# The end of a graph attention kernel: range check moved into the last row group, last accumulators' large halves added from PSUM, last row group stored in four

## The chip, the cores and the metric

One core of a Trainium2 chip. The metric is the device time of one execution in microseconds, the median of several runs. Profile times are microseconds from the start of the span; an engine's idle time stands in square brackets behind an instruction, with what ended it.

## The reference

The input is x, 8192 rows of 128, an adjacency matrix adj of 8192 x 8192 integers 0 or 1 with about 0.2% ones, a 128 x 128 matrix W and a vector a of 256.

```python
h = relu(layernorm(x))
Wh = h @ W
f1, f2 = Wh @ a[:128], Wh @ a[128:]
e = leaky_relu(f1[:, None] + f2[None, :], 0.2)
e = where(adj == 0, -inf, e)
out = x + softmax(e, axis=1) @ Wh
```

## The kernel before

The 8192 rows are 64 tiles of 128 (NB), in 16 row groups of four (NQ = 16, PACK = 4). The columns are walked in 16 units of 512 (UN = 16). The exponentials of the attention are written as a maximum of two products, so that the weight of an edge is the larger of a row factor and a column factor, times the edge's mark; `weights` (line 784) forms them on VectorE, four operations of 128x512 for each unit, reading the row factors from a bank of the PSUM tensor `stage` and writing to `wt_ring`, which holds two units (NW = 8).

TensorE's `unit` waits for a unit's weights and runs `products`: for each of the four row tiles r, eight matmuls (lines 376 and 380) add to `acc[:, r]`, one PSUM bank for each row tile. The factors are kept as a large and a small half in 16 bits: columns 0 to 128 of a bank (E1 = 129: 128 features and the sum of weights) collect the large part, columns 129 to 257 the small one, scaled by LOW = 2048. Ahead of most units stand two transposes of adjacency words (line 365), which ScalarE turns into marks (line 541). VectorE may write the weights of unit u once TensorE has finished unit u - 2 (semaphore `used`).

At the end of a row group ScalarE copies the four accumulators to `fin` (`evacuate`, line 576). For groups 0 to 14 the sum of the two halves, the division and the addition of x run on GpSimd, VectorE and ScalarE beside the next group, and SP stores the group's 256 KB (line 176).

For the last group it is done at once, on VectorE: for each row tile r it waits for ScalarE's copy (`acc_free`), adds the halves (line 880), takes the reciprocal of the sum of weights (line 882) and forms the output in `xm` (line 884). Then SP stores the whole group with one transfer.

The factors of the fast way are only valid for inputs in a certain range. `lim` holds, for each partition, the largest f2, the largest -f2 and a sum of squares. After the last unit TensorE turns it into one partition with three matmuls against the identity (line 457; each runs as two passes); VectorE then reduces these and compares them in four small operations (lines 870 to 874), before it takes up the last group's sums, and writes `flag`. Each engine loads the flag into a register; with these inputs it is 1, and the exact but slow way behind `Else` isn't run. The helper `then` makes VectorE wait until the operation just issued has completed.

The order on each engine is written out by hand, and the engines meet at semaphores. Engine queues: SP stores, GpSimd loads adjacency.

Of the kernel before, what the change touches and what calls it, by code (L numbers as in the profile page):

```python
# [28 lines left out]
ALU = mybir.AluOpType  # L29
ACT = mybir.ActivationFunctionType  # L30
# [8 lines left out]
P = 128  # L39
PACK = 4  # L40
# [19 lines left out]
def gat_kernel(nc, x, adj, W, a, out):  # L60
# [20 lines left out]
    with ExitStack() as ctx:  # L81
# [83 lines left out]
        @block.sync  # L165
        def _(sp):
            def load_x(k):
                lo, hi = BATCHES[k]
                sp.dma_start(xm[:, lo:hi, :], x_dram[:, lo:hi, :]).then_inc(x_loaded[k], 16)

            for k in range(len(BATCHES)):
                load_x(k)

            with sp.Fori(0, NQ) as q:
                sp.wait_ge(s["rows_done"], (q + 1) * PACK)
                sp.dma_start(out_dram[:, q, :], xm[:, q, :]).then_inc(s["out_stored"], 16)
            sp.wait_ge(s["flag_ready"], 1)
            fast = sp.value_load(flag[0:1, 0:1], min_val=0, max_val=1)
            sp.wait_ge(s["out_stored"], 16 * NQ)
            with sp.If(fast):  # L180
                pass
            with sp.Else():
                sp.dma_start(xm[:], x_dram).then_inc(s["x_again"], 16)
                with sp.Fori(0, NQ) as q:
                    sp.wait_ge(s["rows_done"], NB + (q + 1) * PACK)
                    sp.dma_start(out_dram[:, q, :], xm[:, q, :]).then_inc(s["out_stored"], 16)
                sp.wait_ge(s["out_stored"], 16 * 2 * NQ)


        @block.gpsimd  # L190
# [132 lines left out]
        def _(pe):  # L323
# [125 lines left out]
            for b in range(UN):  # L449
# [1 line left out]
                    pe.wait_ge(s["marked"], (NQ - 1) * UN + b + 2)  # L451
                    transposes(b + 2, (NQ - 1) * UN + b + 2)
                unit((NQ - 1) * UN + b, b, NQ - 1)
            pe.wait_ge(s["limits_ready"], 1)
            pe.wait_ge(s["weighted"], NQ * UN * PACK)
            for k in range(3):
                mm = nc.tensor.matmul(stage[0:1, 0, k * P:(k + 1) * P], lim[:, k:k + 1], ident[:],
                                      start=(k == 0), stop=(k == 2), skip_group_check=True)
            mm.then_inc(s["limits_turned"], 1)
            pe.wait_ge(s["flag_ready"], 1)  # L460
            fast = pe.value_load(flag[0:1, 0:1], min_val=0, max_val=1)
            with pe.If(fast):
                pass
            with pe.Else():
                pe.wait_ge(s["acc_free"], NB)
                pe.wait_ge(s["weighted"], NQ * UN * PACK)
                for q in range(NQ):
                    if q >= 4:
                        pe.wait_ge(s["row_ready"], q - 3)
                    for r in range(PACK):  # L470
                        t = q * PACK + r
                        mm = nc.tensor.transpose(acc[:, q % 4, r * P:(r + 1) * P],
                                                 wh[:, t, E1:WC].to_broadcast([P, P]), ident[:])
                    mm.then_inc(s["rowp_ready"], 1)
                pe.wait_ge(s["row_ready"], NQ)
                with pe.Fori(0, NQ) as q:
                    for n in range(GC):
                        c, at = n // PACK, q * GC + n
                        pe.wait_ge(s["g_probs"], at + 1)
                        for k in range(KC):  # L480
                            for r in range(PACK):
                                mm = nc.tensor.transpose(stage[:, k, r * P:(r + 1) * P], scoreq[:, k, r, :], ident[:])
                            mm.then_inc(s["g_tp"], 1)
                        for k in range(KC):
                            pe.wait_ge(s["g_t"], at * KC + k + 1)
                            for r in range(PACK):
                                mm = nc.tensor.matmul(acc[:, 0, 0:Fo], probt[:, k, r * P:(r + 1) * P],
                                                      wh[:, (c * KC + k) * PACK + r, 0:Fo],
                                                      start=(k == 0 and r == 0),
                                                      stop=(k == KC - 1 and r == PACK - 1))  # L490
                        mm.then_inc(s["g_sums"], 1)
# [3 lines left out]
        def _(act):  # L495
# [182 lines left out]
            for b in range(2, UN):  # L678
                steady(NQ - 1, b, more=b + AHEAD < UN)
                if b == 8:  # L680
                    divided(NQ - 2)
            evacuate(NQ - 1)
            act.wait_ge(s["flag_ready"], 1)
            fast = act.value_load(flag[0:1, 0:1], min_val=0, max_val=1)
            with act.If(fast):
# [19 lines left out]
        def _(dve):  # L705
            steps = [0]

            def then(ins):

                steps[0] += 1  # L710
                ins.then_inc(s["dve_step"], 1)
                dve.wait_ge(s["dve_step"], steps[0])
# [117 lines left out]
            for b in range(UN):  # L830
# [12 lines left out]
                if b == 3 or b == 7:  # L843
                    inverses(3 + b // 7)

            def rows(q, bank, more=True):

                dve.wait_ge(s["e_kept"], q)
                if more:
                    next_group(q + 1)  # L850
                for b in range(UN):
                    u = q * UN + b
                    dve.wait_ge(s["marked"], u + 1)
                    dve.wait_ge(s["used"], u - 1)
                    weights(bank, b)
                    if b == 6:
                        dve.wait_ge(s["sums_ready"], q)
                        nc.vector.reciprocal(inv[:], fin[:, :, Fo]).then_inc(s["inv_ready"], 1)

            f2 = wh[:, :, E1]  # L860
            nc.vector.reduce_max(lim[:, 0:1], f2, AX_X)
# [2 lines left out]
            with dve.Fori(0, (NQ - 2) // 2) as p:  # L864
                rows(p * 2 + 1, 2)
                rows(p * 2 + 2, 1)
            rows(NQ - 1, 2, more=False)
            dve.wait_ge(s["limits_turned"], 1)
            square_limits = [v * v / (NORM * D) for v in WH_LIMITS]
            then(nc.vector.reduce_max(glim[0:1, :], stage[0:1, 0, 0:3 * P].rearrange("p (k i) -> p k i", k=3), AX_X))  # L870
            then(nc.vector.tensor_scalar(gs[0:1, 0:1], glim[0:1, 0:1], glim[0:1, 1:2], F2_LIMIT, ALU.max, ALU.is_le))
            then(nc.vector.tensor_scalar(gs[0:1, 1:2], glim[0:1, 2:3], square_limits[1], gs[0:1, 0:1],
                                         ALU.is_le, ALU.mult))
            nc.vector.tensor_scalar(flag[0:1, :], glim[0:1, 2:3], square_limits[0], gs[0:1, 1:2],
                                    ALU.is_ge, ALU.mult).then_inc(s["flag_ready"], 1)

            q = NQ - 1
            for r in range(PACK):
                dve.wait_ge(s["acc_free"], q * PACK + r + 1)
                then(nc.vector.scalar_tensor_tensor(out=fin[:, r, 0:E1], in0=fin[:, r, E1:2 * E1], scalar=1.0 / LOW,  # L880
                                                    in1=fin[:, r, 0:E1], op0=ALU.mult, op1=ALU.add))
                then(nc.vector.reciprocal(inv[:, r:r + 1], fin[:, r, Fo:E1]))
                o = xm[:, q, r * P:(r + 1) * P]
                nc.vector.scalar_tensor_tensor(out=o, in0=fin[:, r, 0:Fo], scalar=inv[:, r:r + 1], in1=o,
                                               op0=ALU.mult, op1=ALU.add).then_inc(s["rows_done"], 1)
# [82 lines left out]
```

## Time and profile before

| | |
|---|---|
| median of 3 runs | 836.5 us (836.43 to 836.5) |
| the profiled execution's own time | 836.72 us |
| its span | 835.1 us |
| TensorE busy (matmul) | 790.1 us, 95% |
| VectorE busy | 758.2 us, 91% |
| ScalarE busy | 487.9 us, 58% |
| GpSimd busy | 411.2 us, 49% |
| granted TensorE clock, mean | 0.991 of full speed |

PE is TensorE's matmuls, PEld its weight loads, DVE is VectorE, ACT ScalarE, POOL GpSimd, SPq SP's queue. The ends of matmuls are modelled: they overlap, so the distance between two starts, not the duration, is the price of one in a stream.

### The profile page before, as it was taken

What the parts mean: (1) busy time and instruction counts of PE and PEld (TensorE: products, weight loads), DVE (VectorE), ACT (ScalarE), POOL (GpSimd) and SP (SyncE); (2) the same over time, 40 slices, a digit from 0 to 9 for tenths busy, and PEclk for the clock granted to TensorE, in tenths of its full rate; (3) what the DMA queues carried; (4) which work ended last, traced back from release to release, by engine and by line L of the source; (5) the groups of instructions that cost most, each with busy time, mean ns of one, the idle gap of its engine ahead of it and who ended that gap; (6) DMA issues with size and microseconds to landing.
All of it is one profiled execution on the core that took longest, in us unless ns stands there. A gap on an engine that the chain in (4) does not pass through costs nothing.

```text
span 835.1 us, 22635 instructions
## 1 busy us (share of the span) xinstructions
PE 790.1 (95%) x8969; PEld 722.9 (87%) x8969; DVE 758.2 (91%) x1243; ACT 487.9 (58%) x793; POOL 411.2 (49%) x606
## 2 busy tenths in 40 slices
PE   3578989999999999999999999999999999999995
PEld 2467879999999999999999999999999999999995
DVE  4699999999999999999999999999999999999995
ACT  4477975555565555555565555555565556555541
POOL 4655656554554446554554446554554446553410
PEclk9899999999999999999999999999999999999998
DMA  9997579999999999999999999999999999997200
GB/s 222 116 108 69 51 73 105 105 87 98 98 90 101 88 107 87 101 87 98 96 90 101 87 106 89 101 87 102 95 88 101 87 109 84 103 86 80 27 15 16
DMA packets 43281, 75.99 MB, mean 91 GB/s; under 512 B 4720, under 2 KB 6896, under 8 KB 43248
## 3 DMA queue, kind: packets, MB, share of 16 engines
q0 software_dynamic: 38400, 67.13, 87.2%
q1 hardware_dynamic: 4432, 8.39, 2.9%
q8 instruction: 17, 0.28, 0.1%
q10 hardware_dynamic: 416, 0.07, 0.0%
q14 instruction: 16, 0.13, 0.0%
HBM read 272.70 MB, written 4.19 MB: 332 GB/s over the span
## 4 chain that ended last, share of the span: by engine, by line
PE 85%; DVE 7%; DMA 4%; ACT 2%; issue 1%; POOL 1%; ACTq 0%; DVEq 0%; POOLq 0%
PE acc L376 51%; PE acc L380 26%; PE stage L365 6%; DMA masks<-in_adj_dram 4%; DVE wt_ring L784 4%; DVE pairs L774 1%; DVE packed L766 1%; PE stage L356 1%; DVE stats L719 1%; ACT masks L559 0%; DVE packed L765 0%; PE stage L348 0%; ACT marks L541 0%; ACT wh L519 0%; ACT pairs L596 0%
## 5 line engine op out<-in xcount | busy, mean ns | idle before, releaser
L784 DVE SCALAR_TENSOR_TENSOR wt_ring<-stage,packed,marks 128x512 f32<-128x512 f32 x1024 | 697.7, 744 | 47.9 <-PE acc L380 41.9
L376 PE MATMUL acc<-pairs,wt_ring 128*128 128x258 f16 x4096 | 721.2, 274 | 9.1 <-DVE pairs L774 8.7
L380 PE MATMUL acc<-pairs,wt_ring 128*128 128x129 f16 x4096 | 699.6, 219 | 0.0
L376 PEld LDWEIGHTS acc<-pairs,wt_ring 128*128 128x128 f16 x4096 | 396.9, 97 | 65.1 <-issue 8.6
L541 ACT ACTIVATE marks<-stage 128x1024 uint16<-128x1024 uint8 x256 | 261.9, 1023 | 292.5 <-PE stage L365 291.5
L380 PEld LDWEIGHTS acc<-pairs,wt_ring 128*128 128x128 f16 x4096 | 400.4, 98 | 2.5
L193 POOL DMA_DIRECT2D masks<-in_adj_dram x252 | 137.7, 549 | 329.7 <-PE stage L365 306.7
L215 POOL TENSOR_TENSOR masks<-masks 128x256 int32<-128x256 int32 x256 | 179.5, 738 | 14.5 <-ACT masks L559 13.6
L559 ACT ACTIVATE masks<-masks 128x512 uint16<-128x512 uint16 x252 | 156.4, 622 | 8.3 <-DMA masks<-in_adj_dram 8.3
L365 PE MATMUL stage<-ident,masks 128*128 128x128 f32 x512 | 99.5, 276 | 2.6 <-ACT fin L632 2.0
L365 PEld LDWEIGHTS stage<-ident,masks 128*128 128x128 f32 x512 | 54.2, 142 | 6.3 <-ACT fin L632 2.3
L348 PE MATMUL stage<-wx,ht 128*128 128x130 f32 x128 | 24.9, 325 | 11.1 <-ACT wh L519 10.4
L348 PEld LDWEIGHTS stage<-wx,ht 128*128 128x128 f32 x128 | 19.8, 220 | 13.7 <-ACT wh L519 12.0
L576 ACT ACTIVATE fin<-acc 128x258 f32<-128x258 f32 x64 | 21.2, 388 | 9.5 <-PE acc L376 9.5
L251 POOL TENSOR_TENSOR tmp<-wh,tmp 128x512 f32<-128x512 f32 x15 | 16.3, 1085 | 19.0 <-ACT tmp L532 18.9
L258 POOL TENSOR_SCALAR fin<-fin 128x516 f32<-128x516 f32 x15 | 22.9, 1524 | 0.3
L268 POOL TENSOR_TENSOR xm<-fin,xm 128x512 f32<-128x512 f32 x15 | 18.0, 1203 | 3.0 <-ACT fin L582 2.9
L582 ACT ACTIVATE fin<-fin,inv 128x128 f32<-128x128 f32 x60 | 19.0, 390 | 0.0
L774 DVE SCALAR_TENSOR_TENSOR pairs<-pairs,tmp 128x516 f16<-128x516 f16 x16 | 13.7, 857 | 5.5 <-ACT pairs L596 5.5
L519 ACT ACTIVATE wh<-stage 128x260 f32<-128x260 f32 x32 | 12.2, 381 | 9.9 <-PE stage L348 9.6
L261 POOL TENSOR_TENSOR fin<-fin 128x516 f32<-128x516 f32 x15 | 16.6, 1104 | 1.3
L335 PE MATMUL stage<-ident,xn 128*128 128x128 f32 x64 | 12.0, 321 | 5.3 <-ACT xn L504 5.3
(62 smaller groups left out, 161.1 us busy)
## 6 DMA issues: line engine op xcount, KB each, us to landing
masks<-in_adj_dram POOLq DMA_DIRECT2D x256, 256.0 KB, 7.1
out_dram<-xm SPq DMA_DIRECT2D x16, 256.0 KB, 7.5
xm<-in_x_dram SPq DMA_DIRECT2D x3, 1024.0 KB, 15.5
xm<-in_x_dram SPq DMA_DIRECT2D x1, 768.0 KB, 6.2
xm<-in_x_dram SPq DMA_DIRECT2D x1, 256.0 KB, 3.1
wx<-in_L_gnn_W_dram ACTq DMA_DIRECT2D x1, 64.0 KB, 3.3
a_sb<-in_L_gnn_a_dram ACTq DMA_DIRECT2D x1, 1.0 KB, 6.2
```

What stands on the lines that cost most here:

```text
L193: nc.gpsimd.dma_start(masks[:, c * PACK + r, :], adj_dram[q, r, c]).then_inc(adj_loaded[c] if r < 2 else adj_second[c], 16)
L215: nc.gpsimd.tensor_tensor(edges4[:, c, 0, :, sl], edges4[:, c, 0, :, sl], edges4[:, c, 1, :, sl], ALU.add).then_inc(s["mixed"], 1)
L258: nc.gpsimd.tensor_scalar(fin[:, :, E1:2 * E1], fin[:, :, E1:2 * E1], 1.0 / LOW, None, ALU.mult).then_inc(s["lows_scaled"], 1)
L348: mm = nc.tensor.matmul(stage[:, 3, r * 256:r * 256 + WC], ht[:, g % 2, k:k + P], wx[:], start=(r == 0), stop=(r == 1), skip_group_check=True)
L365: mm = nc.tensor.transpose(stage[:, 0, r * P:(r + 1) * P], words[:, c * PACK + r, kk * P:(kk + 1) * P], ident[:])
L376: return nc.tensor.matmul(acc[:, r, 0:2 * E1], wtv[:, w, r, 1, :], pairv[:, t, :, 0:E1], start=st, stop=end)
L380: return nc.tensor.matmul(acc[:, r, 0:E1], wtv[:, w, r, 0, :], pairv[:, t, 0, 0:E1], start=False, stop=False)
L541: nc.scalar.activation(split[:, b % MR, :].rearrange("p (s w) -> p s w", s=PACK), stage[:, 0, 0:BANK // 2].bitcast(U8).rearrange("p (w s) ...
L559: nc.scalar.activation(twos[:, c, 1, :, sl], twos[:, c, 1, :, sl], ACT.Copy, scale=SECOND).then_inc(s["second_ready"], 1)
L576: nc.scalar.activation(fin[:, r, :], acc[:, r, 0:2 * E1], ACT.Copy).then_inc(s["acc_free"], 1)
L774: nc.vector.scalar_tensor_tensor(out=pairv[:, sl, 1, 0:E1], in0=pairv[:, sl, 0, 0:E1], scalar=-LOW, in1=tmp[:, g % 2], op0=ALU.mult, op1=A ...
L784: nc.vector.scalar_tensor_tensor(out=wtq[:, t % NW], in0=e_row, scalar=packed[:, t, 1:2], in1=edges[:, k], op0=ALU.max, op1=ALU.mult).then ...
```

## The change

The three matmuls that turn the limits stand behind unit 4 of the last row group on TensorE and write to bank 3 of `stage`, which is free by then. The check's four operations on VectorE stand behind the weights of unit 8 of the last group, in a function `check`. ScalarE no longer copies an accumulator of the last group whole: it copies the small half alone, with the scale 1/2048 applied. VectorE adds the large half from PSUM to it. SP loads the flag ahead of the last group's stores and stores that group as four transfers of 64 KB, each when its row tile is done.

```diff
@@ -171,12 +171,16 @@
             for k in range(len(BATCHES)):
                 load_x(k)
 
-            with sp.Fori(0, NQ) as q:
+            with sp.Fori(0, NQ - 1) as q:
                 sp.wait_ge(s["rows_done"], (q + 1) * PACK)
                 sp.dma_start(out_dram[:, q, :], xm[:, q, :]).then_inc(s["out_stored"], 16)
             sp.wait_ge(s["flag_ready"], 1)
             fast = sp.value_load(flag[0:1, 0:1], min_val=0, max_val=1)
-            sp.wait_ge(s["out_stored"], 16 * NQ)
+            for r in range(PACK):
+                sp.wait_ge(s["rows_done"], NB - PACK + r + 1)
+                sl = slice(r * P, (r + 1) * P)
+                sp.dma_start(out_dram[:, NQ - 1, sl], xm[:, NQ - 1, sl]).then_inc(s["out_stored"], 16)
+            sp.wait_ge(s["out_stored"], 16 * (NQ - 1 + PACK))
             with sp.If(fast):
                 pass
             with sp.Else():
@@ -184,7 +188,7 @@
                 with sp.Fori(0, NQ) as q:
                     sp.wait_ge(s["rows_done"], NB + (q + 1) * PACK)
                     sp.dma_start(out_dram[:, q, :], xm[:, q, :]).then_inc(s["out_stored"], 16)
-                sp.wait_ge(s["out_stored"], 16 * 2 * NQ)
+                sp.wait_ge(s["out_stored"], 16 * (2 * NQ - 1 + PACK))
 
 
         @block.gpsimd
@@ -451,18 +455,19 @@
                     pe.wait_ge(s["marked"], (NQ - 1) * UN + b + 2)
                     transposes(b + 2, (NQ - 1) * UN + b + 2)
                 unit((NQ - 1) * UN + b, b, NQ - 1)
-            pe.wait_ge(s["limits_ready"], 1)
-            pe.wait_ge(s["weighted"], NQ * UN * PACK)
-            for k in range(3):
-                mm = nc.tensor.matmul(stage[0:1, 0, k * P:(k + 1) * P], lim[:, k:k + 1], ident[:],
-                                      start=(k == 0), stop=(k == 2), skip_group_check=True)
-            mm.then_inc(s["limits_turned"], 1)
+                if b == 4:
+                    pe.wait_ge(s["limits_ready"], 1)
+                    pe.wait_ge(s["e_kept"], NQ - 1)
+                    for k in range(3):
+                        mm = nc.tensor.matmul(stage[0:1, 3, k * P:(k + 1) * P], lim[:, k:k + 1], ident[:],
+                                              start=(k == 0), stop=(k == 2), skip_group_check=True)
+                    mm.then_inc(s["limits_turned"], 1)
             pe.wait_ge(s["flag_ready"], 1)
             fast = pe.value_load(flag[0:1, 0:1], min_val=0, max_val=1)
             with pe.If(fast):
                 pass
             with pe.Else():
-                pe.wait_ge(s["acc_free"], NB)
+                pe.wait_ge(s["rows_done"], NB)
                 pe.wait_ge(s["weighted"], NQ * UN * PACK)
                 for q in range(NQ):
                     if q >= 4:
@@ -679,7 +684,15 @@
                 steady(NQ - 1, b, more=b + AHEAD < UN)
                 if b == 8:
                     divided(NQ - 2)
-            evacuate(NQ - 1)
+
+            act.wait_ge(s["rows_done"], (NQ - 1) * PACK)
+            for r in range(PACK):
+                if r < PACK - 1:
+                    act.wait_ge(s["acc_done"], (NQ - 1) * (PACK - 1) + r + 1)
+                else:
+                    act.wait_ge(s["used"], NQ * UN)
+                nc.scalar.activation(fin[:, r, E1:2 * E1], acc[:, r, E1:2 * E1], ACT.Copy, scale=1.0 / LOW
+                                     ).then_inc(s["acc_free"], 1)
             act.wait_ge(s["flag_ready"], 1)
             fast = act.value_load(flag[0:1, 0:1], min_val=0, max_val=1)
             with act.If(fast):
@@ -843,6 +856,17 @@
                 if b == 3 or b == 7:
                     inverses(3 + b // 7)
 
+            def check():
+
+                dve.wait_ge(s["limits_turned"], 1)
+                square_limits = [v * v / (NORM * D) for v in WH_LIMITS]
+                then(nc.vector.reduce_max(glim[0:1, :], stage[0:1, 3, 0:3 * P].rearrange("p (k i) -> p k i", k=3), AX_X))
+                then(nc.vector.tensor_scalar(gs[0:1, 0:1], glim[0:1, 0:1], glim[0:1, 1:2], F2_LIMIT, ALU.max, ALU.is_le))
+                then(nc.vector.tensor_scalar(gs[0:1, 1:2], glim[0:1, 2:3], square_limits[1], gs[0:1, 0:1],
+                                             ALU.is_le, ALU.mult))
+                nc.vector.tensor_scalar(flag[0:1, :], glim[0:1, 2:3], square_limits[0], gs[0:1, 1:2],
+                                        ALU.is_ge, ALU.mult).then_inc(s["flag_ready"], 1)
+
             def rows(q, bank, more=True):
 
                 dve.wait_ge(s["e_kept"], q)
@@ -856,6 +880,8 @@
                     if b == 6:
                         dve.wait_ge(s["sums_ready"], q)
                         nc.vector.reciprocal(inv[:], fin[:, :, Fo]).then_inc(s["inv_ready"], 1)
+                    if b == 8 and not more:
+                        check()
 
             f2 = wh[:, :, E1]
             nc.vector.reduce_max(lim[:, 0:1], f2, AX_X)
@@ -865,20 +891,11 @@
                 rows(p * 2 + 1, 2)
                 rows(p * 2 + 2, 1)
             rows(NQ - 1, 2, more=False)
-            dve.wait_ge(s["limits_turned"], 1)
-            square_limits = [v * v / (NORM * D) for v in WH_LIMITS]
-            then(nc.vector.reduce_max(glim[0:1, :], stage[0:1, 0, 0:3 * P].rearrange("p (k i) -> p k i", k=3), AX_X))
-            then(nc.vector.tensor_scalar(gs[0:1, 0:1], glim[0:1, 0:1], glim[0:1, 1:2], F2_LIMIT, ALU.max, ALU.is_le))
-            then(nc.vector.tensor_scalar(gs[0:1, 1:2], glim[0:1, 2:3], square_limits[1], gs[0:1, 0:1],
-                                         ALU.is_le, ALU.mult))
-            nc.vector.tensor_scalar(flag[0:1, :], glim[0:1, 2:3], square_limits[0], gs[0:1, 1:2],
-                                    ALU.is_ge, ALU.mult).then_inc(s["flag_ready"], 1)
 
             q = NQ - 1
             for r in range(PACK):
                 dve.wait_ge(s["acc_free"], q * PACK + r + 1)
-                then(nc.vector.scalar_tensor_tensor(out=fin[:, r, 0:E1], in0=fin[:, r, E1:2 * E1], scalar=1.0 / LOW,
-                                                    in1=fin[:, r, 0:E1], op0=ALU.mult, op1=ALU.add))
+                then(nc.vector.tensor_tensor(fin[:, r, 0:E1], acc[:, r, 0:E1], fin[:, r, E1:2 * E1], ALU.add))
                 then(nc.vector.reciprocal(inv[:, r:r + 1], fin[:, r, Fo:E1]))
                 o = xm[:, q, r * P:(r + 1) * P]
                 nc.vector.scalar_tensor_tensor(out=o, in0=fin[:, r, 0:Fo], scalar=inv[:, r:r + 1], in1=o,
```

## Rows read from the trace of the kernel before

**Rows 1.** The page: busy time by engine, and shares of the chain that ended last.
```profile
PE 790.1 (95%) x8969; PEld 722.9 (87%) x8969; DVE 758.2 (91%) x1243; ACT 487.9 (58%) x793; POOL 411.2 (49%) x606
...
PE 85%; DVE 7%; DMA 4%; ACT 2%; issue 1%; POOL 1%; ACTq 0%; DVEq 0%; POOLq 0%
```

**Rows 2.** Timeline of VectorE, last row group: start, duration, operations [idle before].
```profile
794.09 2.73 DVE L784 SCALAR_TENSOR_TENSOR wt_ring<-stage,packed,marks 128x512 f32<-128x512 f32 x4 [0.18 <-PE acc L380]
796.73 0.17 DVE L858 RECIPROCAL inv<-fin 128x4 f32<-128x4 f32 x1
796.99 2.73 DVE L784 SCALAR_TENSOR_TENSOR wt_ring<-stage,packed,marks 128x512 f32<-128x512 f32 x4
...
814.43 2.73 DVE L784 SCALAR_TENSOR_TENSOR wt_ring<-stage,packed,marks 128x512 f32<-128x512 f32 x4 [0.18 <-PE acc L380]
817.33 2.73 DVE L784 SCALAR_TENSOR_TENSOR wt_ring<-stage,packed,marks 128x512 f32<-128x512 f32 x4 [0.18 <-PE acc L380]
```

**Rows 3.** Timeline of TensorE: transposes and first products of units 13 and 14.
```profile
817.07 0.39 PE L365 MATMUL stage<-ident,masks 128*128 128x128 f32 x2
817.29 0.27 PE L376 MATMUL acc<-pairs,wt_ring 128*128 128x258 f16 x1
...
820.12 0.29 PE L376 MATMUL acc<-pairs,wt_ring 128*128 128x258 f16 x1
```

**Rows 4.** Timeline of the end, all engines.
```profile
823.97 0.39 ACT L576 ACTIVATE fin<-acc 128x258 f32<-128x258 f32 x1 [5.45 <-PE acc L376]
...
825.81 0.82 PE L457 MATMUL stage<-ident,lim 128*1 128x128 f32 x6
825.92 0.39 ACT L576 ACTIVATE fin<-acc 128x258 f32<-128x258 f32 x1 [0.28 <-PE acc L376]
826.66 0.55 DVE L870 TENSOR_REDUCE glim<-stage 1x3 f32<-1x384 f32 x1 [3.70 <-PE stage L457]
...
827.85 0.27 DVE L880 SCALAR_TENSOR_TENSOR fin<-fin 128x129 f32<-128x129 f32 x1
...
828.62 0.28 DVE L880 SCALAR_TENSOR_TENSOR fin<-fin 128x129 f32<-128x129 f32 x1
...
830.72 0.35 DVE L884 SCALAR_TENSOR_TENSOR xm<-fin,inv,xm 128x128 f32<-128x128 f32 x1
831.26 0.34 SPq L176 DMA_DIRECT2D out_dram<-xm  x1
```

**Rows 5.** SP's load of the flag and its last branch: durations in ns, starts.
```profile
L178 SPq TENSOR_LOAD <-flag x1: 707/707/707, 831.8 to 831.8; - x1
...
L180 SPq COMPARE_BRANCH  x2: 34/36/38, 833.6 to 833.7; - x2
```

**Rows 6.** Groups of instructions by line and shape: busy us, mean ns of one.
```profile
L727 DVE TENSOR_TENSOR small<-stats 128x16 f32<-128x16 f32 x3 | 0.5, 181 | 0.0
L728 DVE SCALAR_TENSOR_TENSOR small<-stats 128x16 f32<-128x16 f32 x3 | 0.5, 176 | 0.0
...
L613 ACT ACTIVATE wt<-acc 128x128 f32<-128x128 f32 x1 | 0.3, 278 | 1.7 <-PE acc L403 1.7
...
L820 DVE COPY e_next<-packed 128x4 f32<-128x4 f32 x1 | 0.2, 170 | 0.0
...
L808 DVE COPY wx<-acc 128x1 f32<-128x1 f32 x1 | 0.2, 159 | 2.7 <-PE acc L406 2.7
```

**Rows 7.** DMA engines from 831.1 to 833.4 in 40 slices; the store.
```profile
DMA  0000000000000000066999799799661030000000
...
out_dram<-xm SPq DMA_DIRECT2D x1, 256.0 KB, 2.3
```

**Rows 8.** The page's DMA issues: KB each, median us to landing.
```profile
xm<-in_x_dram SPq DMA_DIRECT2D x1, 768.0 KB, 6.2
xm<-in_x_dram SPq DMA_DIRECT2D x1, 256.0 KB, 3.1
wx<-in_L_gnn_W_dram ACTq DMA_DIRECT2D x1, 64.0 KB, 3.3
```

## What I expect of the change

> **What bounds the kernel now.** I read the page first. TensorE is busy for 95% of the span and holds 85% of the chain that ended last; VectorE is close behind at 91% busy [rows 1]. So almost the whole span is TensorE's, and two questions remain: what does the end look like once TensorE is done, and how much room has VectorE inside the last row group, into which the change moves work.
>
> The second question is answered by the VectorE timeline. A unit's four weight operations take 2.73 us, a unit starts every 2.90 to 2.91 us (814.43 to 817.33), and before each one VectorE waits 0.18 us for TensorE [rows 2]. That 0.18 us is all the room VectorE has: the reciprocal at 796.73 starts 2.64 us after its unit (0.09 us before the last weights are through) and the next unit still starts 2.90 us after the last one, so 0.17 us of foreign work fits in free [rows 2]. TensorE has less room towards VectorE. The weights of unit 13 end at 814.43 + 2.73 = 817.16; unit 14 has no transposes ahead of it, and there TensorE starts 0.06 us after the weights' end (817.33 + 2.73 = 820.06 to 820.12); so it could have begun unit 13 at 817.22 and began at 817.29 [rows 2, 3]. Only 0.07 us lies between the two engines: each bounds the other, and neither can catch up afterwards.
>
> The first question is answered by the timeline of the end. TensorE's last product ends at about 825.88 (ScalarE's fourth copy starts at 825.92). Then come, in a line: the turning of the limits 825.81 to 826.63, the check on VectorE from 826.66, four rounds of sum, reciprocal and output from 827.85 to 831.07, the store at 831.26 [rows 4], its landing and SP's last branch at 833.6 [rows 5], the end at 835.1. So 5.4 us of serial work stand between the last product and the store's issue, and VectorE has nothing to do for 3.70 us before the check [rows 4].
>
> **The change, part by part.**
>
> *1. The limits' matmuls move behind TensorE's unit 4 of the last group.* Six passes, 0.82 us busy for all, of which the last one's own length is 0.27: five starts in 0.55, 0.11 us each [rows 4]. On an engine with no gap, six cost 0.66 us. The same gap is seen for the transposes: two passes start at 817.07 and the next product at 817.29 [rows 3]. Their waits (limits ready, row kept) have long been met. What is queued behind them is units 5 to 15, all of it on the path: **+0.66** (0.55 if one pass hides in the unit's start, 0.82 if nothing overlaps). The release of VectorE's unit 6 lies ahead of them, that of unit 7 behind them; so VectorE merely stands 0.66 us longer before unit 7, and nothing runs in that stand.
>
> *2. The check moves behind VectorE's unit 8.* From its first operation to the start of what follows it takes 827.85 - 826.66 = 1.19 us [rows 4]. It would start 2.64 us after unit 8, as the reciprocal did, and unit 9 after 2.64 + 1.19 = 3.83 instead of 2.90: 0.93 late. TensorE's room takes 0.07 of that: **+0.86**. Queued behind the check are the weights of unit 9, and TensorE waits for these. VectorE makes up 0.25 per unit only until it has to wait for TensorE again, at unit 11, which is itself late; the loss stays. Bounds: 0.70 if the short operations overlap a unit's tail better, 1.15 if their semaphore waits expose more.
>
> *3. At the end, ScalarE copies only the small halves (129 columns for 258) with the scale.* The nearest row is the 128x128 copy out of PSUM, 0.28 us [rows 6], against 0.39 [rows 4]. The first starts at 823.97 on the old scale; with 0.05 us from engine to engine (0.06 above, 0.03 from the limits' end to the check) VectorE can begin at 823.97 + 0.28 + 0.05 = 824.30 instead of 827.85. The fourth is ready at 825.92 + 0.28 + 0.05 = 826.25, before VectorE's fourth round (below), so ScalarE never holds it.
>
> *4. VectorE adds the large half straight from PSUM.* A round now takes 828.62 - 827.85 = 0.77 to 0.79 us; the four with their tail take 831.07 - 827.85 = 3.22 [rows 4]. A tensor_tensor costs what a scalar_tensor_tensor does (181 and 176 ns at 128x16), and an operand in PSUM shows no price (a copy of 128x1 from PSUM 159 ns, of 128x4 from SBUF 170) [rows 6]. I take no change: round 4 starts at 826.67 and the last output ends at 824.30 + 3.22 = 827.52, where it was 831.07: **-3.55**. Upper bound for the new sum: 0.35 each, the time of the output operation with its pointer scalar [rows 4], 0.07 more four times, -3.27.
> The Trainium skill speaks against this part: "VectorE: DVE Perf Modes", in its section on the TRN2 errata, gives a VectorE operation 120 cycles beside its elements with a source in PSUM and 58 with SBUF. That would be an estimated 65 ns for each sum, 0.26 us in all, and the total below would be 0.26 smaller. The trace's two copies do not show such a step.
>
> *5. The last row group is stored in four.* SP has three more issues, each 0.34 us [rows 4] against a round of 0.79, so they don't queue; only the last counts. Its issue needs no register arithmetic of a loop; of the 0.19 us between 831.07 and 831.26 I take **-0.10** (0 to -0.15). The store lands 2.3 us after its issue; in the activity of the 16 engines it moves data over 14 slices of 0.0575 us, some 0.8 us, and the rest is delay before and behind [rows 7]. A quarter of the bytes in pieces of a quarter should take between a quarter and a half of that: **-0.4**. Bounds: -0.6 (in proportion), and 0, since at the start 64 KB in such pieces took 3.3 us and 256 KB took 3.1 [rows 8].
> By the Trainium skill, "DMA: Bandwidth & Descriptors", section on the anatomy of one DMA, a transfer costs about 2 us fixed plus its bytes over 436 GB/s (fitted on GpSimd's transfers), and an estimate from it is 0.60 - 0.15 = 0.45 us saved. No run here shows that fit.
>
> *6. SP's load of the flag* (0.71 us at 831.8 [rows 5]) ran while the store landed, so moving it ahead of the stores gains nothing; it now waits for the flag in the middle of the group, long before its first store. The other engines read theirs while VectorE and the store go on.
>
> **Sum**: 0.66 + 0.86 - 3.55 - 0.10 - 0.40 = -2.53 us. The profiled execution took 836.72 us for a span of 835.1, 0.22 above the median of 836.5. The span should become 832.5, and the median 836.5 - 2.5 = **834.0**. 0.2% of this kernel is 1.67 us, about what a measurement can tell from no change.
>
> **Rivals.**
> *A, the check is hidden in the middle.* If the two engines had real slack, items 1 and 2 cost nothing: -4.05, 832.4 us. For it: VectorE is busy 91%, and the ring holds two units of weights. Against it: the room above, 0.18 and 0.07 us. 7%.
> *B, it is paid fully and the end returns less.* Check at 1.15, matmuls at 0.82, sums at 0.35, no gain at the store: 1.97 - 3.27 = -1.3, 835.2 us; half of that way is already 834.6. For it: at the start a small transfer was no quicker. Against it: all bounds at once. 14%.
> *C, slower: the four stores land one after another.* If each held the queue until it had landed, at 2.3 us apiece, the first issued at 824.30 + 0.85 + 0.15 + 1.52 = 826.8 would be followed by the end of the fourth at 836.0 instead of 833.6: +2.4, 838.9 us. It decides for slower from (833.6 + 1.67 - 826.8) / 4 = 2.1 us per store, and for no gain from 1.7. For it: they share one queue. Against it: the first two loads of x, issued together, took 3.1 and 6.2 us for 256 and 768 KB, though the second was issued behind the first: no full landing stands between them [rows 8]. 4%. The fixed 2 us of the skill's "DMA: Bandwidth & Descriptors" would act so only if stores did not overlap.
> My forecast, each step within its bounds: 75%.
>
> **Numbers.** The likeliest has 834.0, its own range 833.3 to 834.7. The range asked for reaches into A and B: 832.8 to 835.3, leaving out most of A and C and the outermost steps. Faster by over 0.2% (below 834.83): all of the forecast but its upper edge, A, and a third of B, 0.80. Within 0.2%: most of B and that edge, 0.15. Slower: C and what I don't see, 0.05.
>
> **What the changed profile would show.** TensorE: the limits' matmuls between units 4 and 5, unit 5's products 0.6 to 0.7 us later than a unit is apart, and one wait for weights of about 0.8 to 0.9 us before unit 9. VectorE: about 0.8 us of waiting before unit 7, 3.83 between the starts of units 8 and 9, no waiting before unit 10. Last product near 827.4. The first sum about 0.4 us after ScalarE's first half copy starts, rounds 0.79 apart, the last output near 829.0, its store issued 0.1 us later, SP's last branch near 831.1. Wrong would make it: a wait at unit 9 absent (A), rounds above 0.9 us, or a fourth store that lands over 3 us after its issue (C).

## The result, and the profile after

The changed kernel takes 834.0 us at the median of 22 runs; the kernel before takes 834.89 us at the median of the 22 runs that belong to this comparison (the 836.5 above was the median of three of them). The medians are 0.9 us apart and the means 1.7 us. The ratio of the two kernels is 0.998, as that of the means, with a 95% interval of 0.9973 to 0.9987: 1.7 us faster, between 1.1 and 2.3. I had forecast 2.5 us, a ratio of 0.997, which is just outside. Whether the gain is over 0.2%, to which I gave a chance of 0.80, stays undecided: 0.998 lies in the middle of the interval.

The profiled execution has a span of 832.6 us, 2.5 us less than before, exactly the forecast; but 0.7 us of that is no effect of the change. The weights of unit 6 of the last group start at 793.38 here and at 794.09 before [rows 2], and up to there the two programs do the same; the last step of VectorE's first stage, the negation of the limit, already starts 0.7 us apart (117.86 and 118.57). In the thirteen profiles of this study the start of unit 6 lies anywhere from 790.86 to 794.09, and always the same time after that negation. So I compare profiles from the start of unit 6's weights on: 41.0 us to the end of the span before, 39.2 after, 1.8 us less, which agrees with the timed 1.7.

**The middle of the last group.** VectorE's timeline after the change (start, duration, operations, idle before), where [rows 2] show it before:

```profile
793.38 2.73 DVE L797 SCALAR_TENSOR_TENSOR wt_ring<-stage,packed,marks 128x512 f32<-128x512 f32 x4 [0.18 <-PE acc L384]
796.02 0.17 DVE L882 RECIPROCAL inv<-fin 128x4 f32<-128x4 f32 x1
797.17 2.73 DVE L797 SCALAR_TENSOR_TENSOR wt_ring<-stage,packed,marks 128x512 f32<-128x512 f32 x4 [0.98 <-PE acc L384]
800.08 2.73 DVE L797 SCALAR_TENSOR_TENSOR wt_ring<-stage,packed,marks 128x512 f32<-128x512 f32 x4 [0.18 <-PE acc L384]
802.72 0.54 DVE L863 TENSOR_REDUCE glim<-stage 1x3 f32<-1x384 f32 x1
...
803.89 5.34 DVE L797 SCALAR_TENSOR_TENSOR wt_ring<-stage,packed,marks 128x512 f32<-128x512 f32 x8
```

VectorE stands 0.98 us before unit 7, behind TensorE's limits; units 6 and 7 are 3.79 us apart instead of 2.91, 0.88 lost. The check then sits between units 8 and 9, 3.81 us apart, and units 9 and 10 follow one another in one piece. TensorE's timeline shows both losses:

```profile
793.20 0.82 PE L462 MATMUL stage<-ident,lim 128*1 128x128 f32 x6
793.95 0.44 PE L369 MATMUL stage<-ident,masks 128*128 128x128 f32 x2
794.22 0.27 PE L380 MATMUL acc<-pairs,wt_ring 128*128 128x258 f16 x1
...
805.62 0.39 PE L369 MATMUL stage<-ident,masks 128*128 128x128 f32 x2
806.66 0.29 PE L380 MATMUL acc<-pairs,wt_ring 128*128 128x258 f16 x1 [0.65 <-DVE wt_ring L797]
```

The product before the limits started at 793.05. The six passes cost their 0.66, but there is a gap ahead of them (0.15 us from the last product's start to theirs, where 0.06 is usual) and one behind (their 0.66 us are over at 793.86, the transposes start at 793.95), and the first product comes 0.27 us after the transposes instead of 0.22 [rows 3]. Before unit 9 the products start at 806.66 where they could have at 805.62 + 0.22 = 805.84: 0.82 us of waiting for weights.

**The end**, where [rows 4] show it before:

```profile
825.28 0.29 DVE L898 TENSOR_TENSOR fin<-acc,fin 128x129 f32<-128x129 f32 x1 [1.31 <-ACT fin L694]
...
826.08 0.28 DVE L898 TENSOR_TENSOR fin<-acc,fin 128x129 f32<-128x129 f32 x1
...
828.17 0.35 DVE L901 SCALAR_TENSOR_TENSOR xm<-fin,inv,xm 128x128 f32<-128x128 f32 x1
```

ScalarE's fourth copy starts at 826.92 and the last output ends at 828.52: 1.60 us, where it was 831.07 - 825.92 = 5.15 before. That is the forecast -3.55 to the digit, with rounds of 0.78 to 0.80 us.

After that the forecast fails. These are the third and the fourth store, from SP's timeline in two stretches:

```profile
827.76 1.38 SPq L182 DMA_DIRECT2D out_dram<-xm  x1
...
829.19 0.43 SPq L182 DMA_DIRECT2D out_dram<-xm  x1
```

The third issue holds SP for 1.38 us, so the fourth store is issued 0.67 us after the last output, and it lands 2.6 us later. From last output to SP's last branch it takes 3.3 us, where it took 2.5 before. And yet the span ends 4.08 us after the last output, where it ended 4.03 after before. If the store ended it both times, the end would have come 0.8 us later. The view of one line tells what does. Line 81 is that of the block, and DRAIN is each engine's last step there before the engines meet; these are the last three, of the kernel before and then of the changed one (durations in ns, then starts in us):

```profile
L81 PEldq DRAIN  x1: 73/73/73, 832.8 to 832.8; - x1
L81 SPq DRAIN  x1: 7/7/7, 833.8 to 833.8; - x1
L81 DVEq DRAIN  x1: 65/65/65, 834.8 to 834.8; - x1
```

```profile
L81 PEldq DRAIN  x1: 73/73/73, 830.2 to 830.2; - x1
L81 SPq DRAIN  x1: 7/7/7, 832.1 to 832.1; - x1
L81 DVEq DRAIN  x1: 65/65/65, 832.3 to 832.3; - x1
```

The last to arrive is VectorE, both times, and the span ends 0.3 us behind it. Before, it is 1.0 us behind SP; in the changed kernel only 0.2 us. What it does between its last output and there stands in the rows of the flag and of its branch, of the changed kernel:

```profile
L904 DVEq TENSOR_LOAD <-flag x1: 547/547/547, 828.2 to 828.2; - x1
```

```profile
L905 DVEq COMPARE_BRANCH  x2: 47/48/50, 829.1 to 829.2; - x2
```

It loads the flag (0.9 us with the register steps, up to the branches at 829.1 and 829.2), and then 3.1 us pass between the second branch and its DRAIN. Between these two stands only the jump over the instructions of the slow way; that it is what takes the time is tested below. The chain of waits ends at the last output and shows none of this, because nothing of it counts as busy.

### The profile page after: what moved, and what is told of

Its sections match the earlier page's. It is cut to its first block, busy times and chain, and to the rows that moved or that the text cites. A ratio compares the mean times of both kernels' runs of the same rounds, so it can differ in the third digit from the quotient of the medians.

```text
span 832.6 us, 22633 instructions
## 1 busy us (share of the span) xinstructions
PE 790.5 (95%) x8969; PEld 723.0 (87%) x8969; DVE 756.0 (91%) x1243; ACT 487.7 (59%) x793; POOL 411.7 (49%) x606
## 4 chain that ended last, share of the span: by engine, by line
PE 85%; DVE 7%; DMA 4%; ACT 2%; issue 1%; POOL 1%; ACTq 0%; DVEq 0%; POOLq 0%
PE acc L380 51%; PE acc L384 26%; PE stage L369 6%; DVE wt_ring L797 4%; DMA masks<-in_adj_dram 4%; DVE pairs L787 1%; DVE packed L779 1%; PE stage L360 1%; PE stage L352 1%; DVE stats L732 0%; ACT masks L564 0%; ACT marks L546 0%; ACT wh L524 0%; ACT pairs L601 0%; DVE packed L778 0%
```

## Experiments

Eleven kernels, all but one timed against the kernel before. In the table U is the start of unit 6's weights, C the start of ScalarE's fourth copy, L the end of VectorE's last output, E the end of the span; the columns are differences of these in each profile.

| kernel | U to C | C to L | L to E | U to E | ratio to before, 95% |
|---|---|---|---|---|---|
| before | 31.83 | 5.15 | 4.0 | 41.0 | |
| changed | 33.54 | 1.60 | 4.1 | 39.2 | 0.998 (0.9973 to 0.9987) |
| one_store | 33.54 | 1.60 | 4.0 | 39.2 | 0.9986 (0.9975 to 0.9997) |
| copy_whole | 33.54 | 1.71 | 4.1 | 39.4 | 0.9976 (0.9964 to 0.9987) |
| check_last | 32.72 | 1.60 | 3.9 | 38.3 | 0.9967 (0.9954 to 0.9979) |
| check_b6 | 32.72 | 1.59 | 4.0 | 38.3 | 0.9958 (0.9942 to 0.9974) |
| early_four | 33.54 | 1.60 | 2.9 | 38.1 | 0.9962 (0.9949 to 0.9976) |
| early_one | 33.54 | 1.60 | 3.1 | 38.2 | 0.9972 (0.996 to 0.9983) |
| no_jump | 33.54 | 1.61 | 2.6 | 37.7 | 0.996 (0.9946 to 0.9974) |
| best | 32.71 | 1.60 | 3.0 | 37.3 | 0.9953 (0.9939 to 0.9967) |
| store_only | 31.83 | 5.14 | 3.8 | 40.7 | 1.0 (0.9989 to 1.0011) |
| limits_13 | 32.30 | 1.60 | 3.9 | 37.8 | 0.996 (0.9946 to 0.9973) |
| no_pe_jump | 33.54 | 1.60 | 3.9 | 39.0 | one run |

The intervals are 1.2 to 2.7 us wide, so it is the profile's columns that tell the small effects apart; the ratios only confirm their sum. U to C and C to L repeat to 0.01 us where nothing was changed in them. L to E doesn't: it is 3.8 to 4.1 in the kernels in which VectorE still loads the flag behind its last output and jumps, so a difference of 0.3 us in that column isn't read as an effect. Each row of the table rests on one profile.

**The last row group in one store.**

```diff
-            for r in range(PACK):
-                sp.wait_ge(s["rows_done"], NB - PACK + r + 1)
-                sl = slice(r * P, (r + 1) * P)
-                sp.dma_start(out_dram[:, NQ - 1, sl], xm[:, NQ - 1, sl]).then_inc(s["out_stored"], 16)
-            sp.wait_ge(s["out_stored"], 16 * (NQ - 1 + PACK))
+            sp.wait_ge(s["rows_done"], NB)
+            sp.dma_start(out_dram[:, NQ - 1, :], xm[:, NQ - 1, :]).then_inc(s["out_stored"], 16)
+            sp.wait_ge(s["out_stored"], 16 * NQ)
...
```

> The changed kernel with the last row group stored in one transfer of 256 KB again, everything else as changed. In the changed kernel's profile the third of the four stores occupied SP for 1.38 us instead of 0.36, the fourth was issued 0.67 us after the last output, and 3.28 us passed from the last output to SP's last branch, where it was 2.53 before. Theory 1 (the split itself costs: SP is held at an issue behind other stores of the same group): with one store the issue comes 0.1 to 0.2 us after the last output, the landing takes 2.2 to 2.4 us, so 2.5 us from last output to branch, 0.75 us less than changed. Theory 2 (the long issue comes from where SP stands in its instructions, whatever it stores): the one store shows an issue of over 1 us, or the time after the branch, 0.8 us in the changed kernel, grows back to the 1.5 us of before. Under theory 1 the whole kernel gains up to 0.75 us against the changed one (ratio to before 0.997), under theory 2 nothing (0.998).

Both theories were half right, and neither said what matters. SP is quick again, as the first had it: last output 827.07, last branch 829.1, 2.0 us. The kernel gains nothing, as the second had it: the end stays 4.0 us behind the last output. Its rows at the block's line:

```profile
L81 SPq DRAIN  x1: 7/7/7, 829.4 to 829.4; - x1
L81 DVEq DRAIN  x1: 66/66/66, 830.8 to 830.8; - x1
```

SP is there 1.4 us before VectorE. In the changed kernel it is there 3.5 us after the last output, here 2.3: the split costs SP 1.2 us, and the kernel nothing.

**The halves copied and added as before.**

```diff
-                nc.scalar.activation(fin[:, r, E1:2 * E1], acc[:, r, E1:2 * E1], ACT.Copy, scale=1.0 / LOW
-                                     ).then_inc(s["acc_free"], 1)
+                nc.scalar.activation(fin[:, r, :], acc[:, r, 0:2 * E1], ACT.Copy).then_inc(s["acc_free"], 1)
...
-                then(nc.vector.tensor_tensor(fin[:, r, 0:E1], acc[:, r, 0:E1], fin[:, r, E1:2 * E1], ALU.add))
+                then(nc.vector.scalar_tensor_tensor(out=fin[:, r, 0:E1], in0=fin[:, r, E1:2 * E1], scalar=1.0 / LOW,
+                                                    in1=fin[:, r, 0:E1], op0=ALU.mult, op1=ALU.add))
```

> The changed kernel with the parts on ScalarE and the sum undone: ScalarE copies both halves (258 columns, 0.39 us) and VectorE adds them from SBUF with the scale. My theory: with the check gone from the end, this part is worth only the difference of the first copy, 0.39 - 0.28 = 0.11 us, since VectorE's four rounds of 0.79 us follow one another after that either way: last output 5.15 - 3.55 + 0.11 = 1.71 us after the start of ScalarE's fourth copy, ratio to before 0.998. Rival: ScalarE's longer copies hold VectorE in a later round too, or the sum from PSUM is quicker than the one from SBUF: 0.3 us or more.

C to L is 1.71, 0.11 us more, as expected. The sum from SBUF takes what the one from PSUM takes; this is this kernel's first sum, and the changed kernel's stands above at 825.28:

```profile
825.95 0.29 DVE L897 SCALAR_TENSOR_TENSOR fin<-fin 128x129 f32<-128x129 f32 x1 [1.42 <-ACT fin L694]
```

Of the 3.55 us at the end, 3.44 come from the check's leaving the end and 0.11 from the shorter copies.

**VectorE's check behind the last weights, or behind unit 6.**

```diff
-                    if b == 8 and not more:
+                    if b == UN - 1 and not more:
```

> The changed kernel with VectorE's check behind the weights of the last unit (15) instead of unit 8; TensorE's limits stay behind unit 4. VectorE has 1.31 us of idle time there in the changed kernel, and the check takes 1.17 us. My theory (VectorE has no room in the middle, so the check cost TensorE 0.82 us at unit 9): that wait goes, the check fits into the idle time, the first sum still starts 1.31 us after the last weights, and the kernel is 0.8 us faster than changed: ratio to before about 0.997. Rival (the wait at unit 9 is no loss because the last units wait for VectorE anyway, or the check delays the first sum): no gain, 0.998, and a first sum more than 1.5 us after the last weights.

U to C falls by 0.82, the whole wait at unit 9. The first sum still starts 1.31 us after the last weights, and ahead of it VectorE waits 0.15 us for ScalarE behind the check: the check fits.

```diff
-                    if b == 8 and not more:
+                    if b == 6 and not more:
```

> The changed kernel with VectorE's check behind unit 6 instead of unit 8, so that it falls where VectorE stands 0.98 us idle because TensorE runs the limits' matmuls. My theory (each engine follows the other, so the same wait can cover both): of the check's 1.17 us, 0.98 + 0.07 are covered, the reciprocal of 0.2 stands there too, and TensorE loses 0.1 to 0.3 us at unit 7 instead of 0.82 at unit 9: 0.5 to 0.7 us faster than changed, ratio 0.9975. Rival (the check's cost is the same wherever it stands in the group): a wait of TensorE for weights of 0.8 us, now at unit 7, and 0.998.

The same 0.82, better than the 0.5 to 0.7 expected. VectorE's timeline of this kernel:

```profile
792.68 2.73 DVE L797 SCALAR_TENSOR_TENSOR wt_ring<-stage,packed,marks 128x512 f32<-128x512 f32 x4 [0.18 <-PE acc L384]
795.32 0.17 DVE L882 RECIPROCAL inv<-fin 128x4 f32<-128x4 f32 x1
795.41 0.52 DVE L863 TENSOR_REDUCE glim<-stage 1x3 f32<-1x384 f32 x1
...
796.56 5.54 DVE L797 SCALAR_TENSOR_TENSOR wt_ring<-stage,packed,marks 128x512 f32<-128x512 f32 x8
```

Unit 7 starts 3.88 us after unit 6, against 3.79 in the changed kernel without any check there; the 0.09 is nearly all within TensorE's room of 0.07. VectorE would stand idle for TensorE's limits there anyway, and the check fills that time: the two insertions together cost what one of them costs, 0.9 us.

**VectorE's load of the flag before the first sum.**

```diff
             rows(NQ - 1, 2, more=False)
+            dve.wait_ge(s["flag_ready"], 1)
+            fast = dve.value_load(flag[0:1, 0:1], min_val=0, max_val=1)
...
-            dve.wait_ge(s["flag_ready"], 1)
-            fast = dve.value_load(flag[0:1, 0:1], min_val=0, max_val=1)
             with dve.If(fast):
```

This first in the changed kernel with its four stores:

> The changed kernel with one move: VectorE loads the flag between the last weights and the first sum, where it has 1.31 us of idle time, instead of behind the last output. Theory (the way out of VectorE ends the kernel): in all profiles so far the last engine to reach the block's end is VectorE, 3.7 to 3.8 us after its last output: load of the flag and its register steps 0.9 us, then the jump over the slow way, 3.1 us to its DRAIN; SP with its stores is there 0.2 us earlier in the changed kernel. So VectorE reaches its DRAIN 0.9 us earlier, but SP with four stores then is last, and the span ends only 0.1 to 0.3 us sooner relative to the last output (4.05 to 3.8). Rival (the store and its landing end the kernel, VectorE's arrival is coincidence): SP's way stays as it is and the end does not move: 4.05 us from last output to end.

The end comes 1.1 us sooner, not 0.1 to 0.3. VectorE gains 0.2 us more than the 0.9 of the load: its second branch now comes at 828.4, while the last output is still under way (to 828.66), and its DRAIN 2.9 us behind the branch, where it was 3.1. I had taken SP's way for given; it changed too (third issue 0.79 us instead of 1.38, SP at the block's end 2.6 us after the last output instead of 3.6), so that both engines drain at 831.3:

```profile
L81 SPq DRAIN  x1: 7/7/7, 831.3 to 831.3; - x1
L81 DVEq DRAIN  x1: 65/65/65, 831.3 to 831.3; - x1
```

Why SP became quicker I did not isolate.

Then with one store:

> The same early load of the flag, and the last row group stored in one transfer. Theory (VectorE's way out ends the kernel): one store has SP at the block's end 1.4 us ahead of VectorE, so now the whole 0.9 us shows: from the last output to the end of the span 3.1 us instead of 4.03, ratio to before about 0.9968. Rival (store and landing end it, and the end adds what it has always added): 4.0 us as in the other kernels with one store, ratio 0.998.

3.1 us, as expected, and the rival's 4.0 is out. That the figure is met is in part chance. VectorE is there 2.7 us after the last output, 1.1 sooner than with one store alone, and SP is last, since its store took 2.5 us to land where it took 2.0 in one_store:

```profile
L81 DVEq DRAIN  x1: 65/65/65, 831.6 to 831.6; - x1
L81 SPq DRAIN  x1: 7/7/7, 831.8 to 831.8; - x1
```

**Nothing for VectorE to jump over.** One store, and VectorE's body of the slow way left out; it doesn't run with these inputs. (`...` stands for that body.)

```diff
-            fast = dve.value_load(flag[0:1, 0:1], min_val=0, max_val=1)
-            with dve.If(fast):
-                pass
-            with dve.Else():
-                ...
+            dve.value_load(flag[0:1, 0:1], min_val=0, max_val=1)
```

> The changed kernel with one store and without VectorE's slow way: its instructions for inputs out of range are left out (they don't run with these inputs), and VectorE loads the flag behind the last output but has nothing to jump over. Theory (the jump over the slow way costs VectorE 3.1 us, whatever is stored): VectorE's DRAIN comes about 1.2 us after the last output, SP with the landing of the store is last at 2.3 us, and the span ends 2.5 to 2.7 us after the last output instead of 4.03: ratio to before 0.9965. Rival (VectorE's arrival is no cause, or the 3.1 us are a wait at the block's end rather than the jump): no change, 4.0 us.

As expected, VectorE, last in the kernel with the jump, is now early, and SP ends the kernel. VectorE's DRAIN comes 0.6 us after its last output, even sooner than the 1.2 expected. The 3.1 us were the jump and no wait at the block's end.

```profile
L81 DVEq DRAIN  x1: 17/17/17, 829.3 to 829.3; - x1
...
L81 SPq DRAIN  x1: 7/7/7, 831.1 to 831.1; - x1
```

L to E is 2.6 us, 1.4 less than with one store alone and the jump.

**The four stores alone, in the kernel before.** Its diff is the change's part on SP and nothing else.

> The kernel before with nothing but the last row group stored in four. Theory (VectorE's way out ends the kernel, 4.03 us after its last output, not the store): the stores change nothing, 4.0 to 4.1 us from the last output to the end of the span, VectorE the last at its DRAIN, ratio 1.000. Rival (the prediction's own step: a smaller last store lands sooner and ends the kernel 0.5 us sooner): 3.5 us, 0.9994, with SP the last engine.

VectorE is last, SP just ahead of it, since its third store took 1.49 us:

```profile
L81 SPq DRAIN  x1: 7/7/7, 831.2 to 831.2; - x1
L81 DVEq DRAIN  x1: 65/65/65, 831.4 to 831.4; - x1
```

The ratio is 1.0, but its interval would admit the rival's 0.9994 too. What speaks against the rival is the order above, VectorE last; it had SP last. L to E is 3.8 us, between its 3.5 and the 4.0 expected; the jump took 2.9 us here and 3.1 before, which is most of the difference from 4.0.

**TensorE's limits behind unit 13**, with the check behind the last weights.

```diff
-                if b == 4:
+                if b == UN - 3:
```

> The changed kernel with VectorE's check behind the last weights (as in the earlier run with the check there) and TensorE's limits behind unit 13 instead of unit 4. Theory (an engine's insertion costs what exceeds its waits for the other one): behind unit 4 they cost 0.88 us, all of it on the path; ahead of units 14 and 15 TensorE has 0.15 and 0.28 us of waiting for weights anyway, so they cost 0.88 - 0.43 = 0.3 to 0.5 us: from the start of unit 6's weights to ScalarE's fourth copy 32.2 to 32.3 us instead of 32.72, ratio to before 0.996. Rival (the cost is the same wherever they stand): 32.7.

U to C is 32.30, at the upper edge of what was expected: 0.47 above before, where it is 0.89 with the limits behind unit 4 (check_last). TensorE's waits for weights ahead of units 14 and 15, 0.15 and 0.22 us in check_last, are gone here and took most of the rest.

**Nothing for TensorE to jump over.** TensorE's body of the slow way left out of the changed kernel (`...` stands for it).

```diff
-            fast = pe.value_load(flag[0:1, 0:1], min_val=0, max_val=1)
-            with pe.If(fast):
-                pass
-            with pe.Else():
-                ...
+            pe.value_load(flag[0:1, 0:1], min_val=0, max_val=1)
```

> The changed kernel (four stores) with TensorE's slow way left out, which doesn't run with these inputs, so that TensorE has nothing to jump over at its end. In the changed kernel the third store occupied SP for 1.38 us while TensorE was in its jump. Theory (the jump's fetching of instructions holds the store's issue): without it all four stores take SP 0.36 to 0.45 us, and SP reaches the block's end 2.5 to 2.8 us after the last output instead of 3.55. Rival (the number of stores outstanding holds SP): the third or fourth still takes over 0.7 us. Either way VectorE is last and the end stays 4.0 us after the last output.

All four issues are short; the rows are those of this kernel and of the changed one (shortest, median and longest in ns):

```profile
L182 SPq DMA_DIRECT2D out_dram<-xm x4: 340/349/357, 825.3 to 827.7; - x4
```

```profile
L182 SPq DMA_DIRECT2D out_dram<-xm x4: 356/394/1383, 826.2 to 829.2; - x4
```

SP is at the block's end 1.9 us after the last output, sooner than the 2.5 to 2.8 expected, and the end of the kernel is unmoved, 3.9. So four stores alone do not hold an issue. That TensorE's jump alone does is not shown either. This is one profile, and in the four kernels with one store and TensorE's jump, that store was issued 2.3 us after TensorE's second branch and took 0.36 us; in the changed kernel the third issue was still held at that time (827.76 to 829.14, the branch at 826.2). That an issue is held only when the jump and earlier stores of the group come together would fit this, but it isn't shown.

**Three of the gains together.** The changed kernel with `b == 6`, the early load and one store; the computation is whole. The later place of TensorE's limits (limits_13) isn't in it.

> Everything that has shown or should show a gain, with the whole computation kept: check behind unit 6, flag loaded on VectorE before the first sum, last row group in one store, and the sum straight from PSUM. By the profiles: the change itself -1.8 us, the check covered -0.82, VectorE's load off its way out -0.9: -3.5 us against before, ratio 0.9958. Rival: the flag's load delays the first sum (its wait queues before the weights are done), then 0.3 to 0.9 us of it comes back, 0.9965 or more.

The first sum starts 1.31 us after the last weights, as in the changed kernel: the load hides. U to E is 37.3, 3.7 us less than before and 1.9 less than the changed kernel. The ratio is 0.9953, where 0.9958 was expected, and its interval lies wholly below that of the changed kernel: it beats both.

## Why the prediction was right and where it was wrong

The kernel became faster for the reason that was given: work left the end, and about half of it came back in the middle. One step failed, the gain from the stores, and the exact figure was luck.

- *Item 1, limits on TensorE, +0.66*: 0.88, over the upper bound of 0.82. The passes cost what was worked out; two gaps around them and a slower restart added 0.22. At the old place the first of these gaps could be seen too (the last product started at 825.61, the limits at 825.81, where 0.11 us is usual), and I read only the distance between passes.
- *Item 2, the check on VectorE, +0.86*: 33.54 - 31.83 - 0.88 = 0.83. Right, and check_last and check_b6 show that it is a cost of the place. That the loss stays, and where it shows, came as described, down to the missing wait before unit 10.
- *Items 3 and 4, -3.55*: -3.55. The sum from PSUM costs nothing more, as the two small copies suggested. The 120 against 58 cycles of the Trainium skill ("VectorE: DVE Perf Modes", errata section) do not show here: the sum takes 0.28 to 0.29 us from PSUM and 0.27 to 0.29 from SBUF.
- *Item 5, four stores, -0.10 and -0.40*: this is the step that failed. The forecast ended the kernel with the store's landing. It ends with VectorE, which was already 1.0 us behind SP in the kernel before (834.8 and 833.8). Moving SP's part moves nothing until VectorE is out of the way: one_store and store_only show it from both sides. Even SP's own time grew, by the hold of the third issue, and the fourth store took 2.6 us to land, where the whole one took 2.3. Only in no_pe_jump do all four small stores land sooner, in 1.6 us each, where one store of 256 KB took 2.0 to 2.5 us, and there too the end stays. The Trainium skill's fixed 2 us plus bytes over 436 GB/s ("DMA: Bandwidth & Descriptors", section on the anatomy of one DMA, fitted on GpSimd's transfers) gave an estimate of nearly the same gain, which failed for the same reason; its fixed part is not met by SP's stores in no_pe_jump, which landed in less than 2 us.
- *Item 6* held the cause in its last sentence: that the other engines read the flag "while VectorE and the store go on" is true of all but VectorE, whose load and jump come behind its last output. The trace of before had it, in the rows of line 81; I had looked at the waits and the busy time, in which it has no row. [rows 5] showed a part: SP's last branch at 833.7 and the end of the span at 835.1, with 1.4 us between them that the prediction left without a cause.
- *The sum*: 0.88 + 0.83 - 3.55 + 0 = -1.84 instead of -2.53; measured -1.8 in the profiles and -1.7 timed. That the predicted 834.0 was met to the digit is luck. The baseline it started from, 836.5, was 1.6 us above the median of the fuller set, and the gain was forecast too large, by 1.6 us against the difference of the medians and 0.8 against that of the means; the two errors cancelled.
- *The rivals*: A (hidden in the middle) is out, by the two losses. B's size, -1.3, is nearer to what was measured than my own -2.53, and two of its four steps came true: the limits on TensorE cost even more than its 0.82, and the store gave nothing. The other two did not: the check cost 0.83 and not 1.15, and the sums no more than before. 14% was too little for it. C is out as stated (the stores overlap: issued at 826.19 to 829.19, landed by 831.8), and a hold of the third store of another kind took its place.

## What to carry to other kernels

Where the chain of waits ends at the last output but the span goes on for microseconds, list every engine's last steps: a load of a flag and a jump over code that doesn't run can be the end of the kernel, as the 0.9 and 3.1 us on VectorE were here, and a faster store is then worth nothing. Where two engines wait for each other with less than 0.2 us between them, put inserted work of both where one covers the other, or in the stretch where one of them waits anyway. And compare profiles from a point behind the noisy part: here the first 120 us moved the whole by up to 3.2 us, more than the change did.

## What the runs showed of the hardware that I had not expected

- VectorE's jump over its slow way took 2.9 to 3.2 us between its branch and its DRAIN, and TensorE's 3.4 to 4.0; SP's and ScalarE's took 0.2 and 0.5 us. Without VectorE's body behind the jump its DRAIN came 0.6 us after the last output's end (828.73 to 829.3), the load of the flag included. The rows are those of the kernel before, VectorE's and TensorE's; the time of TensorE's jump stands in its second branch (3661 ns):

```profile
L888 DVEq COMPARE_BRANCH  x2: 47/48/50, 831.6 to 831.7; - x2
```

```profile
L462 PEldq COMPARE_BRANCH  x2: 66/1864/3661, 828.9 to 829.1; - x2
```

- Two DMA queues carry instructions, with 17 and 16 packets over the span in every kernel but two: without TensorE's body the first has 15, without VectorE's the second has 15. That fits jumps that fetch instructions from memory; how much of a jump's time the fetch takes no run shows.
- While TensorE's jump was under way, SP's issue of a store took up to 1.49 us instead of 0.36 (1.38, 1.24, 1.25, 0.83, 0.79 and 1.49 in six kernels with four stores; at most 0.36 in the one profile without the jump). Packets of instructions stand in the same stretch of the DMA view (two in the changed kernel from 827.0 to 829.2), but whether the issue waits for such a packet or for an earlier store held up by it stays open.
- In limits_13, with TensorE's jump in the same place relative to the stores, the third issue took 0.34 us and the longest, the fourth, only 0.54. So the hold varies, and nothing here says with what.
